# Decoder block on one core: the fp16 high parts of four more experts per group are cast on ScalarE instead of VectorE

## The reference

```python
x = layernorm(x + linear_attention(x))              # 16 heads, gelu'd q and k, rotary, gamma/beta norm inside
x = layernorm(x + cross_attention(x, ctx_1024))     # 16 heads of 8, softmax over 77 context rows
x = layernorm(x + moe_ffn(x))                       # 16 experts, top 4, hidden 256, exact gelu
# moe_ffn, dense over the experts:
for e in range(16):
    hmid = gelu(x @ w1[e] + b1[e])
    out += (hmid @ w2[e] + b2[e]) * combine[:, e]   # combine is zero for experts not chosen
```

## Time and profile before

| | us |
|---|---|
| median of 3 runs (lowest, highest) | 619.71 (618.11, 620.84) |
| the profiled execution | 618.64 |
| its span, first to last instruction | 616.8 |
| PE busy | 578.8 (94%) |
| DVE busy | 445.3 (72%) |
| ACT busy | 405.0 (66%) |
| POOL busy | 314.0 (51%) |

### The profile page before, as it was taken

How to read it: one execution, slowest core, us unless ns; L and a number is a source line. 1 busy time by engine, 2 the same in 40 slices (tenths; PEclk the granted TensorE clock), 3 DMA queues, 4 the chain that set the end, 5 groups by cost and what they waited for, 6 DMA issues and landing times. The chain is left out here.

```text
span 616.8 us, 17220 instructions
## 1 busy us (share of the span) xinstructions
PE 578.8 (94%) x6780; PEld 414.5 (67%) x6780; DVE 445.3 (72%) x1504; ACT 405.0 (66%) x520; POOL 314.0 (51%) x199
## 2 busy tenths in 40 slices
PE   6798888999999999999999999999999988899994
PEld 2544644777677877777677767786677756585664
DVE  2467476758897888888887889788878886267456
ACT  1425754796659765886579666976588657866661
POOL 5165432646357444665357544834566536155553
PEclk9898997999999999999999999999999999899999
DMA  6540111010200030002100120003000110000000
GB/s 179 157 138 27 46 49 43 5 30 1 72 14 10 2 91 28 22 2 62 56 21 3 46 73 19 4 2 108 10 22 3 35 55 4 2 19 2 2 18 18
DMA packets 31607, 23.08 MB, mean 37 GB/s; under 512 B 2808, under 2 KB 30216, under 8 KB 31528
## 3 DMA queue, kind: packets, MB, share of 16 engines
q1 hardware_dynamic: 23801, 16.59, 9.2%
q10 hardware_dynamic: 7375, 4.97, 2.7%
q0 software_dynamic: 352, 0.43, 0.4%
HBM read 13.90 MB, written 5.46 MB: 31 GB/s over the span
## 5 line engine op out<-in xcount | busy, mean ns | idle before, releaser
L540 POOL TENSOR_TENSOR gl<-g,gh 128x1024 f16<-128x1024 f32 x96 | 204.1, 2135 | 176.3 <-ACT gh L705 104.3
L716 ACT ACTIVATE g<-ps,b 128x512 f32<-128x512 f32 x256 | 168.5, 686 | 91.8 <-PE ps L1003 90.4
L1372 DVE SCALAR_TENSOR_TENSOR acc<-ps,cw,acc 128x128 f32<-128x128 f32 x448 | 125.9, 344 | 67.6 <-PE ps L1024 50.9
L1022 PE MATMUL ps<-w2h,gh 128*128 128x128 f16 x768 | 133.6, 219 | 1.9 <-DVE acc L1372 1.5
L1024 PE MATMUL ps<-w2h,gl 128*128 128x128 f16 x768 | 133.4, 219 | 0.0
L1023 PE MATMUL ps<-w2l,gh 128*128 128x128 f16 x768 | 133.4, 219 | 0.0
L1001 PE MATMUL ps<-x2h,w1h 128*128 128x512 f16 x256 | 98.6, 385 | 4.8 <-ACT g L716 4.8
L1003 PE MATMUL ps<-x2h,w1l 128*128 128x512 f16 x256 | 98.0, 383 | 0.0
L1002 PE MATMUL ps<-x2l,w1h 128*128 128x512 f16 x256 | 98.0, 383 | 0.0
L1022 PEld LDWEIGHTS ps<-w2h,gh 128*128 128x128 f16 x768 | 75.1, 98 | 18.1 <-issue 10.8
L1023 PEld LDWEIGHTS ps<-w2l,gh 128*128 128x128 f16 x768 | 75.1, 98 | 5.4 <-issue 1.6
(11 more groups left out here) (189 smaller groups left out, 900.2 us busy)
## 6 DMA issues: line engine op xcount, KB each, us to landing
q_rep<-q_parts SPq DMA_DIRECT2D x24, 128.0 KB
x<-in_x SPq DMA_DIRECT2D x8, 256.0 KB, 3.6
w_stage<-in_L_ffn_w ACTq DMA_DIRECT2D x1, 2048.0 KB, 10.9
q_swap<-q SPq DMA_DIRECT2D x16, 128.0 KB, 2.1
q_parts<-qx SPq DMA_DIRECT2D x16, 128.0 KB, 2.1
k_rep<-k_parts SPq DMA_DIRECT2D x24, 77.0 KB
out<-fin SPq DMA_DIRECT2D x7, 256.0 KB, 2.5
g<-in_L_ffn_w ACTq DMA_DIRECT2D x6, 256.0 KB, 3.1
```

The source lines that it names most:

```text
L540: pool.tensor_tensor(gl[:, j % SPLIT_RING, :, :], g32[:, e % RING, :, :], gh[:, j % SPLIT_RING, :, :], ALU.subtract).then_inc(s["lo"], 1)
L716: act.activation(g32[:, e % RING, h, :], bH[:, h, :], ACT.Gelu, bias=b1[:, e, h:h + 1], scale=1.0 / WS).then_inc(s["gelu"], 1)
L1022: pe.matmul(o, ghb, w2h[:, j, h, :], start=(h == 0), stop=False)
L1372: m = dve.scalar_tensor_tensor(out=(acc_all if e == E - 1 else acc)[:, b, :], in0=second_bank(f, e)[:, b * P:(b + 1) * P], scalar=cw[:, b, ...
```

## The change

All twelve split experts are cast by ACT, at the same place (3 of each expert) as before; the DVE's `high` is removed with its table entries and its semaphore, and POOL's `low` waits for the one count that is left.

```diff
-BY_VECTOR = tuple(range(2, E, 4))
-BY_SCALAR = tuple(e for e in SPLIT if e not in BY_VECTOR)
-DVE_AT = dict(high=3, q=23, ...
+DVE_AT = dict(q=23, ...
-DVE_ZERO = dict(high=3, q=2, ...
+DVE_ZERO = dict(q=2, ...
             def low(f, e):
                 j = SPLIT.index(e)
-                if e in BY_VECTOR:
-                    since(pool, "hi_ve", len(BY_VECTOR) * f + BY_VECTOR.index(e) + 1)
-                else:
-                    since(pool, "hi", len(BY_SCALAR) * f + BY_SCALAR.index(e) + 1)
+                since(pool, "hi", len(SPLIT) * f + j + 1)
@@ ACT body
-                        if f is not None and p % PLACES == at["high"] and e in BY_SCALAR:
+                        if f is not None and p % PLACES == at["high"] and e in SPLIT:
                             high(f, e)
@@ DVE
-            def high(f, e):
-                j = SPLIT.index(e)
-                since(dve, "gelu", HALF * (E * f + e + 1))
-                if j >= SPLIT_RING:
-                    since(dve, "y_p", E * f + SPLIT[j - SPLIT_RING] + 1)
-                else:
-                    since(dve, "y_p", E * (f - 1) + SPLIT[j - SPLIT_RING] + 1)
-                dve.tensor_copy(gh[:, j % SPLIT_RING, :, :], g32[:, e % RING, :, :]).then_inc(s["hi_ve"], 1)
@@ DVE body
-                        if f is not None and p % PLACES == at["high"] and e in BY_VECTOR:
-                            high(f, e)
```

More of the change, by code:

```diff
@@ L90 @@
               weights=0, c_t=61, gelu=1, high=3, u=(40, 45), ao_t=52)
-DVE_AT = dict(high=3, q=23, kv01=17, kv23=22, k_rot=26, k_mean=26, kv=31, den=33, out=33, norm1=37, norm2=41,
+DVE_AT = dict(q=23, kv01=17, kv23=22, k_rot=26, k_mean=26, kv=31, den=33, out=33, norm1=37, norm2=41,
               x1=49, v1=47, k=57, q_x=63, scores=(5, 8, 9, 11, 15, 16, 20, 20), max=22, pairs=(42, 47), wo=55,
@@ L116 @@
                norm2=26, k=38, x1=35, q_x=62, xl=0)
-DVE_ZERO = dict(high=3, q=2, kv01=8, kv23=16, k_rot=25, k_mean=24, kv=27, den=29, out=29, norm1=31, norm2=38,
+DVE_ZERO = dict(q=2, kv01=8, kv23=16, k_rot=25, k_mean=24, kv=27, den=29, out=29, norm1=31, norm2=38,
                 x1=46, v1=45, k=56, q_x=63, scores=(4, 5, 10, 11, 11, 16, 18, 18), max=20, pairs=(43, 44),
@@ L284, in build @@
             lg_p lg top topx cut chosen lgm th num dnm rdn pm ps_ cw cwh cwl cw_tp cw_tc b2_p acc_b2
-            h_p gelu hi hi_ve lo y_p comb st4 ve4 rs4 fin
+            h_p gelu hi lo y_p comb st4 ve4 rs4 fin
             y_half end_sum end_st end_ve end_rs end_fin""".split()
```

## The result

| | before | after |
|---|---|---|
| median of 10 runs, us (lowest, highest) | 618.28 (613.89, 621.19) | 624.68 (623.05, 630.22) |
| ratio to before, 95% interval | | 1.0126 (1.0094 to 1.0157) |
| the profiled execution, us | 618.64 | 624.25 |
| its span, us | 616.8 | 622.4 |

The ten runs of before include the three that the forecast was made against. Against the forecast of 622.6 us the sign is right and the range (618.8 to 627.0) holds the time, but the forecast loss was 2.9 us and the measured one is some 6 to 8 us. More than half of it is not in the sum.

What follows compares the result with a forecast made beforehand. PE, busy 94% of the span, was taken as the bound. Terms 2.4 (expert 10, groups 1 to 5) + 0.28 (group 6) + 0.2 (group 0) = 2.9 us, on 619.7 gave 622.6 us; range 618.8 to 627.0.

Steps and rivals of the forecast that it cites:

- Where the bound was: PE, busy 94% of the span, sets the time; what counts is when it stands still.
- The DVE casts: Removing 32 casts, 22.3 us of DVE busy time, gains 0, since DVE waits for PE behind them anyway.
- Expert 10: ACT's cast before the next gelu delays the u copy; PE's transposes wait 0.48 us in groups 1-5, 0.28 in group 6.
- Expert 6: ACT's cast pushes mx_t back 0.47 us, covered by slack; cost 0, bounds 0 to 0.29 us a group.
- Experts 2 and 14 on ACT: Behind their gelus ACT waits 1.90 and 1.52 us for PE, so the cast's 0.93 us fits; cost 0.
- Group 0, expert 6: The cast before the first exponential makes transposed scores late; 0.2 us taken, bounds 0 and 0.52.
- What it moves: the start of POOL's low parts: Low parts wait for ACT's cast and may start earlier; nobody gains, as PE wants them three experts later.
- rival C: Faster: POOL's 0.5 us on kr reaches PE, 618.6 us; chance 0.10 together with an unseen DVE gain.
- Rival A: Slower by more: late gelus of experts 11 or 7 reach PE in full, 7.0 to 7.9 us; chance 0.20 with variant.
- Its variant: PE's stall drops the clock to 1.2 GHz, costing 1 us a time; in six groups 629 us.
- The expected signs: In the changed profile: ACT near 438 us, DVE near 423, u wait about 0.5, period 66.9, kr 1.27 us.

Runs made afterwards that it cites:

- e4: Changed kernel, but POOL's low part of expert 14 waits for x2n and ACT's cast of expert 10 follows the second u copy; 617.46 us, ratio 0.9984.
- e5: Kernel before without the casts of experts 2, 6, 10 and 14 from group 1 on, POOL's low part waiting for the gelu; 624.08 us, one run.
- e7: Kernel before with the casts of experts 2 and 6 alone moved to ACT; 617.43 us, one run.
- e3: Kernel before with the cast of expert 10 alone moved to ACT; 621.01 us, ratio 1.0063.
- e1: Changed kernel, but POOL's low part of expert 14 waits until the four x2n instructions are done; 620.49 us, ratio 1.0064.
- e6: Changed kernel, but POOL does the low part of expert 14 in two half-size instructions; one run, period 67.49 us.

## Why the prediction was right in direction and short in size

*Where the bound was.* Right: PE's waits, not any engine's busy time. ACT went from 66 to 70% at no cost in itself (e4, at 71%).

*The DVE casts, 0.* Right: e5 and e7.

*Expert 10.* Right in place and in size. Forecast 0.48 us for each of groups 1 to 5 and 0.28 in group 6, measured 0.41 to 0.43 and 0.23; the load went at 341.48 without a wait before and follows the copy's end by 0.06 us now. The cast started 0.30 us after `cx_t`, as worked out. e3 gives it alone.

*Expert 6.* Right. `mx_t` comes 22.16 us after the group's tanh instead of 21.78, 0.38 us later (forecast 0.47), and the scores behind it do not wait. *Experts 2 and 14 on ACT* are hidden, as forecast: the idle time before the next gelu fell from 1.90 to 0.82 and from 1.52 to 0.45 us.

*Group 0, expert 6.* The transposed scores wait 0.36 us for the exponential, and a later wait on DVE's `kv` shrank from 0.59 to 0.35 us, which leaves 0.12. The 0.2 us that I took is about right.

*The step that failed* is the second: "What it moves: the start of POOL's low parts ... Nobody gains". It asked who could gain by an earlier low part and not what an earlier low part would meet. I had the mechanism on the table, since I weighed the rule of the Trainium skill (SBUF — State Buffer, Who interferes with whom) on exactly these two engines. But I used it in one direction only, for the DVE instruction that goes (the cast that had held up `kr`) and not for the DVE instructions that stay. The same section of the Trainium skill says that whichever of the two starts first has the port for the whole instruction. The trace of after agrees: 1.50 us instead of 0.34, to within 0.1 us of POOL's end. And the kernel before had an instance which I had read past. DVE, then POOL, group 2:

```profile
332.99 1.31 DVE L1118 TENSOR_SCALAR ve<-mv 128x4 f32<-128x4 f32 x1
...
332.14 2.13 POOL L540 TENSOR_TENSOR gl<-g,gh 128x1024 f16<-128x1024 f32 x1 [0.57 <-ACT gh L705]
```

This `ve`, four elements wide, takes 0.17 us where no low part runs beside it; here it took 1.31 and ended at 334.30, 0.03 us after POOL's low part of expert 9. Nobody on PE waited for it. Two more in each of groups 1 to 5 (0.61 and 0.24 us) also end 0.02 to 0.03 us after a low part. With the row shown the sum could have been made: low part of expert 14 from the end of `rstd` (354.11) to 356.24, first `x2n` due at 354.79, so it ends at about 356.3 instead of 355.13, some 1.2 us late. The transposes were loaded at 356.32 without a wait, and the fourth `x2n` had ended at 355.90, so 0.4 us were spare: 0.7 to 0.8 us a group. That is what was measured.

*The gain on `kr`*, rival C: POOL's `kr` has a median of 1.27 us now instead of 1.77, and PE gains nothing by it, since its wait on `kr` stands at 1.1 us. The rule and the trace agree in size and the rival still gave nothing.

*Rival A* had the larger loss (627 us) for another reason, late gelus passed on in full. PE's wait on the gelu grew by only 0.5 us, so A's mechanism is not what happened. Its variant had the price of a fall of the clock too low: the one in group 6 before cost some 1.7 us, as worked out above, not 1.

*The expected signs:* DVE near 423 us was wrong (440.7); 10.7 us of that gap are the blocked `x2n`. The period was to be 66.9 and is 67.60. It has grown by 1.18 us, beyond the 0.9 us that the prediction had named as a sign that it is wrong; what the prediction would have read as rival A was the blocked `x2n`. The clock did not fall in groups 1 to 5.

*Luck.* That the range holds the time owes something to luck: the range reached up to 627 for A's late gelus, which did not come, and the forecast started from a median of three runs that lies 1.4 us above that of all ten. From 618.28 the same sum gives 621.2, and the measured time is 3.5 us above it, more than the forecast change itself.

*The sum with the missing term.* 1.18 x 5 = 5.9 us for groups 1 to 5. In group 6 the waits are 0.73 and 0.23 us, but about 0.5 came out of them: 62.88 us against the 62.40 of e4, both at full clock. In group 0 the wait of 3.0 us came out as 2.1 to 2.6, an estimate from two pairs. Against the kernel before the group is 0.57 us longer, and at the granted clock of 0.80 and 0.61 over 8 us of it the execution before lost some 1.5 us more to the clock: 2.1. Against e1, whose group 0 has full clock and no wait on `x2n` (66.40 us), the 70.58 us of after, less the 1.6 us that its own clock cost, are 2.6 us longer. Together 8.5 to 9.0 us, or 1.4 to 1.5%, against a measured 1.26% (0.94 to 1.57%). Where the rest of the waits in groups 0 and 6 is made good was not followed.

## What to carry to other kernels

When a step moves to another engine, its end moves too; follow what that end releases, and look at which instructions of other engines the released work now runs beside. An accidental order (here: POOL could not start until DVE had passed `x2n`, because the cast stood behind it in DVE's list) can protect a critical instruction, and when the dependency goes, an explicit wait may have to take its place. On an engine that other engines wait for, place filler work behind the instruction that is waited for, not at the nearest idle time.

## What was not expected of the hardware

A DVE `tensor_scalar` on 128x128 elements with source and result in SBUF took 1.50 us instead of 0.34 when it started 0.71 us into a GpSimd `tensor_tensor` of 2.13 us, and one on 128x4 took 1.31 us instead of 0.17. A `tensor_tensor` with two sources in SBUF (`cw`, 128x64) took 0.73 instead of 0.22 us in groups 1 to 5 and ended 0.08 us after POOL. Under the same kind of GpSimd instruction, DVE instructions that read PSUM (0.53 us for `kx`) and a batch-norm aggregate (four in 0.38 us) kept their times. Of two GpSimd instructions in a row each held DVE anew, and one DVE instruction came through at the boundary: in e6 the first `x2n`, and in group 0 of the changed kernel, where the second low part came 0.10 us behind the first, the second `x2n` (0.33 us) before the third was held for 2.14 us, 4.44 us for the four. The blocked time is counted as busy, so a DVE that is held up looks like a DVE that works.
